# The dense stage inside attention B's loop, and elu + 1 without VectorE

## The chip, the cores and the metric

The kernel runs on one core of a Trainium2 chip. The metric is the device time of one execution in microseconds; the time before is the median of three runs. A profiled execution gives one more time, the span from the first to the last instruction, and the trace that all rows below come from.

## What is computed

Three blocks run in sequence on a batch of 32 sequences of 256 tokens with 128 features (`NB, T, P = 32, 256, 128`). Attention A ends with a linear layer, a residual, a layer norm and a two-layer MLP; an FFN of eight experts is folded into one 128 x 128 matrix per pair of sequences; attention B is an infini-attention with 16 heads of 8 features and segments of 64 tokens.

```python
# end of attention A ("dense")
out = res + _lin(out, Wf, bf)
res2 = out
on = _ln(out, g2, b2)
ffn = _lin(jax.nn.relu(_lin(on, Wr1, br1)), Wr2, br2)
return res2 + ffn

# attention B, one segment of 64 tokens, _sigma(x) = elu(x) + 1
sq = _sigma(q)
denom_q = jnp.sum(sq * z[:, :, None, :], axis=-1, keepdims=True) + EPS
A_mem = jnp.matmul(sq, M) / denom_q
scores = jnp.matmul(q, jnp.swapaxes(k, -2, -1)) * inv_sqrt_dk
scores = jnp.where(causal, -jnp.inf, scores)
A_dot = jnp.matmul(jax.nn.softmax(scores, axis=-1), v)
A_s = beta * A_mem + (1.0 - beta) * A_dot
sk = _sigma(k)
V_prev = jnp.matmul(sk, M) / denom_k
M_new = M + jnp.einsum('bhtk,bhtv->bhkv', sk, v - V_prev)
```

## The kernel before, in words

`program` calls three functions in turn, each with its own buffers, its own eight PSUM banks at most and a block of its own, and the next starts when the one before has ended: `attention_a`, `dense`, `attention_b`. They hand over through DRAM: `dense` reads the scratch tensors `y` and `ao` of attention A and the input `x`, and writes `x2`; `attention_b` reads `x2` and the folded matrices.

Every function writes one program per engine. The order of the work on an engine is the order of the code, and semaphores alone tie engines together. `pipeline` calls `body(j, u)` for one unit after another, the first and last ones written out and the middle in a loop; `active(j, u, lag)` says whether the unit `n - lag` exists, so one body holds parts of several units at different stages.

`dense` (16 units of 512 rows, names with `b_`) goes per unit: transpose `ao` (L1058), copy to `ao_t`, matmul with `Wf` into `r` (L1089, L1156), moments and norm (GpSimd, L963 to L969), normalise `z` (L1014), transpose, scale to `on`, matmul to `h` (L1099), relu to `hid` (L1042), matmul to `f` (L1112), `x1` = f + residual (L1137), a second layer norm `z1`, its transpose, the matmul with the folded FFN matrix (L1075), `x2` (L1148). Each of the intermediate results has a PSUM bank of its own.

`attention_b` (32 units of one sequence, names with `c_`) has bodies of eight steps `s`. In each step TensorE does, for one head pair g: T, the causal mask and negated row maxima (L1586) plus two heads' scores (L1591) into `t_ps`, which ScalarE turns into `prob` by exp (L1506), and one step later P times V into `c_o_bank` (L1641). At s = 1, 2, 4 and 5 a first pass of scores (L1606, L1611) goes to VectorE's row maximum (L1800), whose three bf16 parts come back through a transpose (L1712). At s = 0 to 2 of unit n the normalised x2 is transposed, multiplied to k and q (L1692, L1693) and copied to `kq` by ScalarE (L1530, L1531, the second with the factor 1/sqrt(8)). GpSimd splits `kq` into three bf16 parts (L1441 to L1444), which go to DRAM and back as the stacks `q_st` and `k_st`. The memory matrix is updated and read at s = 1 to 6 (L1671, L1677) with VectorE's divisions between (L1829, L1831, L1834, L1838). At s = 7 VectorE divides P times V by its row sums (`dinv` L1919, `ad` L1923), and three bodies later than kq come the output projection (`x3`, L1888), a layer norm, the folded matrix again (L1721) and the output (`x4`, L1906).

elu + 1 is computed as max(x, 0) + exp(min(x, 0)): VectorE takes both from PSUM (L1897, L1898), ScalarE the exp (L1546), GpSimd the sum `sg` (L1456).

`free` makes a PSUM bank's next user wait for the last reader of the user before; `USES_A` and `USES_B` list the users of a shared bank in their order within a body.

## Time and profile before

| | us |
|---|---|
| median of 3 runs (lowest, highest) | 1620.86 (1620.09, 1623.54) |
| profiled execution, its own time | 1616.4 |
| its span, first to last instruction | 1614.6 |
| attention A, up to the first load of the dense stage | 781 |
| dense stage, up to the first load of attention B | 177 |
| attention B | 657 |
| mean granted TensorE clock, share of full speed | 0.96 |

In the rows, PE is TensorE's matmul, PEld its weight load, DVE is VectorE, ACT ScalarE, POOL GpSimd. A duration includes the pipeline's latency, so neighbouring instructions of one engine overlap; a difference of two starts tells what one costs. The granted clock is 1.00 at 2.4 GHz and 0.50 at 1.2 GHz. An f32 matmul is two passes and stands as two instructions, a transpose as one.

### The profile page before, as it was taken

How to read it: one execution, taken by the hardware profiler on the slowest of the kernel's cores; microseconds unless marked ns; L12 is line 12 of the kernel's file. 1: busy time of each engine (PE TensorE's matmuls, PEld its weight loads, DVE VectorE, ACT ScalarE, POOL GpSimd, SP SyncE). 2: the span in 40 equal slices, each digit the busy share in tenths (PEclk: the TensorE clock that was granted, in tenths of full speed). 3: DMA queues.
4: the chain of work that ended last, by engine and by line, in shares of the span. 5: the costliest groups of instructions: out<-in, count | busy, mean ns of one | idle time of the engine just before them, and what ended most of it. 6: DMA issues, size and time to landing. Idle time of an engine off the chain costs nothing. (4 is left out here: it accounts for less than half of the span.)

```text
span 1614.6 us, 48196 instructions
## 1 busy us (share of the span) xinstructions
PE 1404.6 (87%) x14500; PEld 1210.9 (75%) x14564; DVE 1121.4 (69%) x3202; ACT 872.3 (54%) x2020; POOL 925.1 (57%) x1340
## 2 busy tenths in 40 slices
PE   5999999999999999999387745899899989998886
PEld 4899899898998999999266633677677766776765
DVE  4468778787888888786344535777777777777764
ACT  2466666666666666666166633444444444444441
POOL 4457676677766777764488834444444444444441
PEclk8899999999999999999599977999999999999996
DMA  4523332323322233321344413343444333333430
GB/s 133 154 86 103 99 88 81 85 88 97 97 77 79 88 97 97 87 75 30 104 115 121 117 55 92 112 108 116 115 116 111 104 104 114 110 114 116 113 101 17
DMA packets 181695, 158.13 MB, mean 98 GB/s; under 512 B 12529, under 2 KB 163185, under 8 KB 181618
## 3 DMA queue, kind: packets, MB, share of 16 engines
q1 hardware_dynamic: 181618, 157.17, 34.2%
q8 instruction: 40, 0.66, 0.2%
q14 instruction: 37, 0.30, 0.1%
HBM read 113.09 MB, written 44.04 MB: 97 GB/s over the span
## 5 line engine op out<-in xcount | busy, mean ns | idle before, releaser
L609 PE MATMUL a_bank<-a_vp,a_prob 128*128 128x74 f32 x4096 | 598.0, 253 | 0.0
L609 PEld LDWEIGHTS a_bank<-a_vp,a_prob 128*128 128x128 f32 x4096 | 587.8, 192 | 5.5
L697 DVE TENSOR_REDUCE a_nmax<-a_bank 128x2 f32<-128x512 f32 x512 | 344.9, 685 | 153.6 <-PE a_bank L578 153.3
L496 ACT ACTIVATE a_prob<-a_bank 128x512 f32<-128x512 f32 x512 | 305.3, 596 | 206.1 <-PE a_bank L593 200.8
L578 PE MATMUL a_bank<-a_k_st,a_q_st 96*128 96x256 bf16 x1024 | 260.5, 278 | 34.9 <-DVE a_nmax L697 24.4
L593 PE MATMUL a_bank<-a_q_st,a_k_st 120*128 120x256 bf16 x1024 | 281.5, 275 | 1.8 <-POOL a_q_st L345 1.8
L1641 PE MATMUL c_o_bank<-c_vb,c_prob 128*128 128x96 f32 x1024 | 178.7, 298 | 17.8 <-DVE c_ad L1923 13.9
L416 POOL TENSOR_TENSOR a_prod<-a_ov,a_wgt 128x512 f32<-128x512 f32 x128 | 151.7, 1185 | 34.1 <-POOL a_prod L416 17.2
L345 POOL TENSOR_SCALAR a_q_st<-a_mt 24x2048 bf16<-24x2048 bf16 x64 | 121.4, 1896 | 85.1 <-ACT a_mt L470 42.2
L1506 ACT ACTIVATE c_prob<-c_bank 128x256 f32<-128x256 f32 x256 | 98.8, 386 | 129.3 <-PE c_bank L1591 127.7
L578 PEld LDWEIGHTS a_bank<-a_k_st,a_q_st 96*128 96x128 bf16 x1024 | 130.7, 135 | 46.2 <-DVE a_nmax L697 32.7
L1641 PEld LDWEIGHTS c_o_bank<-c_vb,c_prob 128*128 128x128 f32 x1024 | 136.8, 194 | 34.2 <-DVE c_ad L1923 18.3
L593 PEld LDWEIGHTS a_bank<-a_q_st,a_k_st 120*128 120x128 bf16 x1024 | 140.1, 137 | 10.6 <-issue 2.2
L1441 POOL TENSOR_SCALAR c_parts<-c_kq 128x512 bf16<-128x512 f32 x32 | 19.8, 618 | 162.5 <-ACT c_kq L1531 162.5
L505 ACT COPY a_ov<-a_bank 128x292 f32<-128x292 f32 x256 | 101.6, 397 | 19.0 <-POOL a_prod L416 17.6
L1800 DVE TENSOR_REDUCE c_nmax<-c_bank 128x8 f32<-128x512 f32 x128 | 88.2, 689 | 21.2 <-PE c_bank L1611 17.7
L1423 POOL TENSOR_SCALAR c_vb<-c_vs 64x128 f32<-64x128 f32 x128 | 38.7, 302 | 96.3 <-PE c_o_bank L1641 63.3
L1591 PEld LDWEIGHTS c_bank<-c_q_st,c_k_st 128*64 128x64 bf16 x2048 | 53.0, 112 | 51.1 <-issue 39.9
L1591 PE MATMUL c_bank<-c_q_st,c_k_st 128*64 128x64 bf16 x2048 | 81.7, 203 | 0.0
L740 DVE TENSOR_REDUCE a_ao<-a_prod 128x128 f32<-128x1024 f32 x64 | 77.3, 1209 | 4.3 <-POOL a_prod L416 4.3
L1611 PE MATMUL c_bank<-c_k_st,c_q_st 128*64 128x64 bf16 x2048 | 57.0, 199 | 21.0 <-issue 16.3
L1586 PE MATMUL c_bank<-c_late,c_pick 88*128 88x256 bf16 x256 | 72.2, 282 | 0.0
(207 smaller groups left out, 2773.2 us busy)
## 6 DMA issues: line engine op xcount, KB each, us to landing
a_q_st<-scratch_a_parts_dram SPq DMA_DIRECT2D x64, 288.0 KB
a_k_st<-scratch_a_parts_dram SPq DMA_DIRECT2D x192, 96.0 KB
c_q_st<-scratch_c_parts_dram SPq DMA_DIRECT2D x64, 288.0 KB
c_k_st<-scratch_c_parts_dram SPq DMA_DIRECT2D x192, 96.0 KB
scratch_a_parts_dram<-a_parts SPq DMA_DIRECT2D x32, 384.0 KB, 2.7
scratch_c_parts_dram<-c_parts SPq DMA_DIRECT2D x32, 384.0 KB, 2.7
a_x<-in_x SPq DMA_DIRECT2D x32, 128.0 KB, 2.9
scratch_y<-a_y SPq DMA_DIRECT2D x32, 128.0 KB, 2.6
```

Source lines behind the costliest of these rows:

```text
L345: pool.tensor_scalar(q_st[o][MROW:AROWS, hs, :], mt[half_][MROW:AROWS, :].unsqueeze(1).broadcast_to([AROWS - MROW, H // 2, T]), 1.0, 0.0, ...
L416: pool.tensor_tensor(prod[o][:, gs, :].rearrange("p g (e r) -> p g e r", r=R), ov[o][:, gs, 0:RD].rearrange("p g (e r) -> p g e r", r=R), ...
L496: act.activation(prob[h % 4][:, :, :].rearrange("p a b -> p (a b)"), t_ps[h % 2][:, :], ACT.Exp).then_inc(exped, 1)
L505: act.copy(ov[(i + lag) % 2][:, 4 * g:4 * g + 4, :], o_ps[g % 2][:, 0:4 * VC].rearrange("p (g c) -> p g c", g=4)[:, :, 0:CQ]).then_inc(ov_ ...
L578: mm = pe.matmul(s_ps[t][:, hh * T:(hh + 1) * T], q_st[o][0:MROW, 2 * g + hh, t * P:(t + 1) * P], k_st[o][0:MROW, 2 * g + hh, :], start=Tr ...
L593: mm = pe.matmul(t_ps[h % 2][:, c * T:(c + 1) * T], k_st[o][0:AROWS, h, c * P:(c + 1) * P], q_st[o][0:AROWS, h, :], start=True, stop=True)
L609: mm = pe.matmul(o_ps[g % 2][:, at:at + VM], prob[h % 4][:, c, t * P:(t + 1) * P], vp[o][:, c, 0:VM], start=c == 0, stop=c == NT - 1)
L697: dve.tensor_reduce(nmax[:, t, 2 * g:2 * g + 2, 0], s_ps[t][:, :].rearrange("p (h k) -> p h k", h=2), AX.X, ALU.max, negate=True).then_inc ...
L1506: act.activation(prob[g % 4][:, :], t_ps, ACT.Exp).then_inc(exped, 1)
L1591: mm = pe.matmul(t_ps[hh * SEG:(hh + 1) * SEG, cs], k_st[st][:, 2 * g + hh, cs], q_st[st][:, 2 * g + hh, cs], start=False, stop=True, skip ...
L1641: mm = pe.matmul(o_ps[:, t, at:at + WIN], prob[g % 4][:, t * P:(t + 1) * P], vb[st][:, t, at:at + WIN], start=True, stop=True)
L1800: dve.tensor_reduce(nmax[:, t, h2 * H // 2:(h2 + 1) * H // 2], s_ps[t][:, :].rearrange("p (h k) -> p h k", h=H // 2), AX.X, ALU.max, negat ...
```

## The change

`dense` is gone as a function. Its work is written into the bodies of `dense_and_attention_b`, in units of 256 rows (one sequence), up to four bodies ahead of attention B: with `E1, E2, E3 = -4, -3, -2`, body n does the first third of unit n + 4, the second of n + 3 and the last of n + 2, and B's first layer norm takes `x2` from SBUF where it read DRAM before. The pipeline starts five bodies early (`AHEAD = 5`). All seven dense matmul and transpose groups share one PSUM bank, `d_ps`, in steps s = 1 to 7, one group a step; for that bank `c_o_bank` shrinks from two banks to one.

P times V: per head pair four matmuls, one for each segment of 64 tokens (64 stationary and 54 moving columns, even segments to output partitions 0 to 63, odd to 64 to 127), where two of 128 and 96 columns stood. The division after it is one reciprocal and one multiplication over all 128 partitions; GpSimd copies `vb` in two pieces where it took four. The factor 1/sqrt(8) moves from the copy of q into the exp, and `kq` is one copy. elu + 1 becomes max(x, 0) + min(exp(x), 1): ScalarE takes exp of `kq`, GpSimd max, min and the sum.

```diff
-        VP = 2 * 2 * (HD + 1)
-        WIN = 96
+        VP = 2 * (HD + 1)
+        WIN = 3 * VP
+        d_ps = ctx.enter_context(nc.psum_tensor("b_bank", [P, 512], F32))
-        o_ps = ctx.enter_context(nc.psum_tensor("c_o_bank", [P, NT, 512], F32))
+        o_ps = ctx.enter_context(nc.psum_tensor("c_o_bank", [P, NT, 256], F32))
+        E1, E2, E3 = -4, -3, -2
+        USES_D = [(aot_d, 1, E1), (on_d, 1, E2), (r_d, 1, E1), (hid_d, 2, E2), (z1t_d, 1, E3), (x1_d, 1, E2),
+                  (x2_d, 1, E3)]
# SyncE, at the head of a body
+                if active(j, u, -AHEAD):
...
+                    sp.dma_start(ao[1 - i][:, :, :], ao_dram[at[0], at[1]]).then_inc(ay_in, 16)
+                    sp.dma_start(dy[1 - i][:, :, :], dy_dram[at[0], at[1]]).then_inc(ay_in, 16)
+                    sp.dma_start(dx[1 - i][:, :, :], dx_dram[at[0], at[1]]).then_inc(dx_in, 16)
...
+                if active(j, u, -1):
+                    sp.wait_ge(x2_d, n + 2)
...
+                    sp.dma_start(x2_dram[at[0], at[1]], x2[1 - i][:, :, :]).then_inc(x2_out, 16)
# GpSimd: norm(0, n + 1) and dxb now at the head of a body, then vb, yb, the split, norm(1, b), and
+                    pool.tensor_scalar(pos[:, :, :], kq[i][:, :, :], 0.0, 0.0, ALU.max, ALU.add).then_inc(sg_n, 1)
                     pool.wait_ge(nexp_d, n + 1)
+                    pool.tensor_scalar(one[:, :, :], nexp[:, :, :], 1.0, 0.0, ALU.min, ALU.add).then_inc(sg_n, 1)
+                    pool.wait_ge(sg_n, 2 * (n + 1))
...
+                if active(j, u, E1):
+                    pool.tensor_tensor(xr[i][:, :, :], dx[i][:, :, :], rows(b_r2[:, :]), ALU.add).then_inc(xr_d, 1)
+                    dense_norm(0, e)
+                    pool.wait_ge(r_d, e + 1)
+                    pool.tensor_tensor(xr[i][:, :, :], xr[i][:, :, :], r[i][:, :, :], ALU.add).then_inc(xr_d, 1)
+                if active(j, u, E2):
+                    dense_norm(1, e)
# ScalarE
-                        act.copy(kq[i][:, 0, :], ps_a[:, 0:T]).then_inc(kq_d, 1)
-                        act.mul(kq[i][:, 1, :], ps_a[:, T:2 * T], HD ** -0.5).then_inc(kq_d, 1)
+                        act.copy(kq[i][:, :, :].rearrange("p a t -> p (a t)"), ps_a[:, :]).then_inc(kq_d, 1)
-                        act.wait_ge(pn_d, (n + 1) * 2)
+                        act.wait_ge(kq_d, n + 1)
-                        act.activation(nexp[:, :, :], neg[:, :, :], ACT.Exp).then_inc(nexp_d, 1)
+                        act.activation(nexp[:, :, :], kq[i][:, :, :], ACT.Exp).then_inc(nexp_d, 1)
# TensorE
-                        for t in range(NT):
+                        for c in range(NS):
                             at = g * VP
-                            mm = pe.matmul(o_ps[:, t, at:at + WIN], prob[g % 4][:, t * P:(t + 1) * P],
-                                           vb[st][:, t, at:at + WIN], start=True, stop=True)
+                            mm = pe.matmul(o_ps[c % 2 * SEG:(c % 2 + 1) * SEG, c // 2, at:at + WIN],
+                                           prob[g % 4][:, c * SEG:(c + 1) * SEG],
+                                           vb[st][:, c, at:at + WIN], start=True, stop=True)
# seven groups after P times V: s = 1 ao, s = 2 z, s = 3 r, s = 4 h, s = 5 z1, s = 6 f, s = 7 g; one of them:
+                    if s == 7 and active(j, u, E3):
+                        e = n - E3
+                        pe.wait_ge(z1t_d, e + 1)
+                        pe.wait_ge(dwc_in, (e + 1) * 16)
+                        free(pe, USES_D, 6, j, u)
+                        for t in range(NT):
+                            mm = pe.matmul(d_ps[:, t * P:(t + 1) * P], z1t[i][:, t * P:(t + 1) * P], dwc[i][:, 0, :],
+                                           start=True, stop=True)
+                        mm.then_inc(dg_p, 1)
# VectorE: r and its moments at s = 3, x1 and its moments at s = 6 behind x4, x2 at s = 7 behind ad
-                        dve.tensor_scalar(flat(pos), ps_a[:, :], 0.0, None, ALU.max).then_inc(pn_d, 1)
-                        dve.tensor_scalar(flat(neg), ps_a[:, :], 0.0, None, ALU.min).then_inc(pn_d, 1)
+                        dve.tensor_tensor(flat(x1[o]), d_ps[:, 0:T], flat(xr[o]), ALU.add).then_inc(x1_d, 1)
+                        dense_moments(1, e, x1[o])
+                        dve.reciprocal(dinv[:, :, :], out[:, :, :, HD]).then_inc(ad_d, 1)
+                        dve.wait_ge(ad_d, AD * b + 1)
+                        dve.tensor_tensor(ad[:, :, :].rearrange("q t (h e) -> q t h e", e=HD), out[:, :, :, 0:HD],
+                                          dinv[:, :, :].unsqueeze(3).broadcast_to([P, NT, H, HD]), ALU.mult
+                                          ).then_inc(ad_d, 1)
+                        dve.tensor_tensor(flat(x2[i]), d_ps[:, 0:T], flat(dxb[i]), ALU.add).then_inc(x2_d, 1)
-    dense(nc, d)
-    attention_b(nc, d)
+    dense_and_attention_b(nc, d)
```

## Rows read from the trace of the kernel before

**Rows 1.** The page's busy line, whole span: busy us, share of span, instructions.
```profile
PE 1404.6 (87%) x14500; PEld 1210.9 (75%) x14564; DVE 1121.4 (69%) x3202; ACT 872.3 (54%) x2020; POOL 925.1 (57%) x1340
```

**Rows 2.** Busy time by stretch: us, busy per engine, granted clock, DMA share, GB/s.
```profile
781.00:957.90 176.90, 126.32 (x768) 95.96 (x768) 72.48 (x304) 99.15 (x208) 130.07 (x193) 0.91 0.38 110
1041.97:1553.36 511.39, 461.17 (x5887) 357.73 (x5941) 382.39 (x1319) 233.81 (x595) 240.93 (x432) 1.00 0.39 111
1553.36:1614.62 61.26, 45.97 (x489) 35.36 (x491) 32.25 (x109) 15.27 (x39) 12.40 (x21) 0.77 0.16 44
```

**Rows 3.** ScalarE in order of time: start us, us, instruction (idle before it).
```profile
968.12 0.37 ACT L1530 COPY c_kq<-c_bank 128x256 f32<-128x256 f32 x1 [2.16 <-PE c_bank L1693]
985.62 0.37 ACT L1530 COPY c_kq<-c_bank 128x256 f32<-128x256 f32 x1 [4.71 <-PE c_bank L1693]
```

**Rows 4.** The waits, 1041.97 to 1553.36 us: waited in total, times, longest.
```profile
PE c_bank L1712 <- DVE c_mpart L1790: 13.0, 27, 0.5
PE c_o_bank L1641 <- DVE c_ad L1923: 12.6, 24, 0.5
PE c_bank L1671 <- DVE c_am L1838: 9.1, 27, 0.4
```

**Rows 5.** Chain that ended last, one body of B: start us, us, what.
```profile
1266.75 0.25 issue
1267.00 0.44 PE c_bank L1611 x16
1267.44 0.61 PE c_o_bank L1641 x4
```

**Rows 6.** TensorE in order of time, the same body.
```profile
1280.24 0.45 PE L1677 MATMUL c_bank<-c_mz,c_sg 128*128 128x144 f32 x2
1280.52 0.61 PE L1721 MATMUL c_bank<-c_wc,c_z4t 128*128 128x128 f32 x4
1280.97 0.27 PE L1586 MATMUL c_bank<-c_late,c_pick 88*128 88x256 bf16 x1
1281.42 0.69 PE L1641 MATMUL c_o_bank<-c_vb,c_prob 128*128 128x96 f32 x4
```

**Rows 7.** VectorE in order of time, the same body.
```profile
1269.92 0.69 DVE L1897 TENSOR_SCALAR c_pos<-c_bank 128x512 f32<-128x512 f32 x1 [1.25 <-ACT c_kq L1531]
1273.31 0.49 DVE L1760 BATCH_NORM_STATS2 c_stats<-c_x 128x6 f32<-128x128 f32 x2
1273.76 0.40 DVE L1764 BATCH_NORM_AGGREGATE c_mv<-c_stats 128x2 f32<-128x6 f32 x2
1280.72 0.17 DVE L1829 TENSOR_SCALAR c_dn<-c_bank 128x16 f32<-128x16 f32 x1 [0.52 <-PE c_bank L1677]
1281.78 0.42 DVE L1906 TENSOR_TENSOR c_x<-c_bank,c_xb 128x256 f32<-128x256 f32 x1
1282.14 0.74 DVE L1919 RECIPROCAL c_dinv<-c_o_bank 64x32 f32<-64x32 f32 x2
1282.92 1.01 DVE L1923 TENSOR_TENSOR c_ad<-c_o_bank,c_dinv 64x128 f32<-64x128 f32 x4
```

**Rows 8.** By tile: count, duration ns min/median/max, first and last start us.
```profile
L1058 PE MATMUL b_bank<-b_ident,b_ao x64: 272/273/476, 786.0 to 926.5; 128*128 128x128 f32 x64
L1148 DVE TENSOR_TENSOR b_x<-b_bank,b_xb x16: 691/692/692, 817.3 to 954.3; 128x512 f32<-128x512 f32 x16
L1760 DVE BATCH_NORM_STATS2 c_stats<-c_x x128: 273/282/297, 961.1 to 1606.3; 128x6 f32<-128x128 f32 x128
```

**Rows 9.** GpSimd in order of time, the same body.
```profile
1270.16 0.62 POOL L1441 TENSOR_SCALAR c_parts<-c_kq 128x512 bf16<-128x512 f32 x1 [5.01 <-ACT c_kq L1531]
1277.47 0.73 POOL L1465 TENSOR_TENSOR c_xb<-c_x,c_wc 128x256 f32<-128x256 f32 x1
1278.28 0.19 POOL L1400 TENSOR_SCALAR c_var<-c_mv 128x2 f32<-128x2 f32 x1
1279.61 0.20 POOL L1407 TENSOR_TENSOR c_shift<-c_negm,c_rs 128x2 f32<-128x2 f32 x1
```

More of the change, by code:

```diff
@@ L55, in pipeline @@
         body(n // 2, n % 2)
-    end = total // 2 - ahead
+    end = (total - ahead) // 2
     with eng.Fori(PEELED // 2, end) as j:
@@ new lines, in body @@
+                    if s == 5 and active(j, u, E3):
+                        e = n - E3
+                        act.wait_ge(z1t_p, e + 1)
+                        if later(j, e, 2):
+                            act.wait_ge(dg_p, e - 1)
+                        act.copy(z1t[i][:, :], d_ps[:, 0:T]).then_inc(z1t_d, 1)
+                    if s == 7 and active(j, u, E1):
+                        e = n - E1
+                        if later(j, e, 2):
+                            act.wait_ge(dzt_p, e - 1)
+                        dense_normed(0, e, r[i], dz[i], dz_d)
@@ new lines, in body @@
+                    if s == 5 and active(j, u, E3):
+                        e = n - E3
+                        pe.wait_ge(z1_d, (e + 1) * NT)
+                        free(pe, USES_D, 4, j, u)
+                        for t in range(NT):
+                            mm = pe.transpose(d_ps[:, t * P:(t + 1) * P], z1[i][:, t, :], ident[:, :])
+                        mm.then_inc(z1t_p, 1)
+                    if s == 6 and active(j, u, E2):
+                        e = n - E2
+                        pe.wait_ge(hid_d, 2 * (e + 1))
+                        free(pe, USES_D, 5, j, u)
+                        for t in range(NT):
+                            for c in range(2):
+                                mm = pe.matmul(d_ps[:, t * P:(t + 1) * P], hid[o][:, c, t * P:(t + 1) * P],
+                                               w_r2[:, c, :], start=c == 0, stop=c == 1)
+                        mm.then_inc(f_p, 1)
```

633 lines of the change are left out of this document (260 added, 373 removed).

## Prediction

> **What bounds the kernel now.** I read four views in this order. First the page's busy line [rows 1]: TensorE is busy for 87% of the span, so time is bought by less TensorE work or by stages in which it waits. Then the stretches [rows 2]: attention A takes the first 781 us, the dense stage has 176.9 us for itself with TensorE busy 126 of them (71%), and attention B follows to the end. Third, the eviction that starts a batch in B's loop (the copy into kq): the first is at 968.1 us, the last at 1553.36, and 27 batches lie between 1041.97 and 1553.36 [rows 2, 3], so the loop's period is 511.39 / 27 = 18.94 us. In that stretch TensorE is busy 461.2 of 511.4 us (90%), VectorE 382.4 (75%), ScalarE 46%, GpSimd 47% [rows 2]. Fourth, the waits there [rows 4]: TensorE waits in three places, for ad (12.6 us), for am (9.1) and for the row maxima's parts (13.0), per batch 0.47 + 0.34 + 0.48 = 1.29. So B's loop is bound by TensorE's order, with about 17.65 us of work per batch and 1.29 of waits for VectorE.
>
> The change therefore moves a stage that TensorE fills badly into one that it fills well. It can win only where the loop grows by less per batch than 176.9 / 32 = 5.5 us plus what the edges give.
>
> **The dense stage in the loop, TensorE.** Per batch of 256 rows: six transposes of 128 columns, eight f32 matmuls of 128 columns (2 for r, 4 for f, 2 for g), two of 256. Two f32 matmuls of 128 columns are four passes and take 1280.97 - 1280.52 = 0.45 from start to start [rows 6], 0.22 each; one of 256 columns is as long as two. A transpose is one pass (x64 for 16 units of four, rows 8), 0.11. Sum 6 x 0.11 + 8 x 0.22 + 2 x 0.44 = 3.3 us. Seven groups each begin after a semaphore; nothing before shows such a start alone. Bounds: nothing, if the sequencer runs ahead, and 0.25 each (1.75), the length of an "issue" piece in the chain [rows 5]. I take 0.25 in all, nearer to nothing, because the groups in rows 6 start without a gap after those before.
>
> **The dense stage, VectorE.** Three adds out of PSUM at 0.42 (x4's, 256 columns) and twice two statistics with their aggregates, 1273.31 to 1274.16, 0.85 [rows 7]: 1.27 + 1.7 = 3.0 us added.
>
> **elu + 1.** The max and min on VectorE go, two of 0.69 that overlap a little, some 1.3 us [rows 7]. They stand right behind the wait for kq, and the reductions, am and the maxima's parts queue behind them, for which TensorE waits. The min's work moves behind ScalarE's exp, which takes the same 512 columns as now; exp now waits for kq alone, and kq is one 512-column copy in place of two. GpSimd gets two one-input operations of 512 columns, 0.62 each by its split of kq [rows 9], and their semaphores. The sum sg is needed only by the next batch's first transposes, several us later: hidden. With these 1.3 us gone, I take the waits for am and for the parts (0.82 us) as gone: r's add and statistics come in between at s = 3, but TensorE has r, the v matmuls and the h matmuls there too.
>
> **The output of P times V.** Before, two f32 matmuls per head pair with 128 stationary and 96 moving columns, 0.61 us of the chain [rows 5], eight times. Now four with 64 and 54 columns, even and odd segments in different halves of the array. Sixteen score matmuls with 64 columns take 0.44 us in the chain [rows 5], 0.028 each, load included, which I read as two halves working at once. For f32 in that form no row exists. Upper bound: eight passes one after another, each 64/128 of the present 0.61 / 4 = 0.15 or somewhat more, again 0.61 and up to 0.07 more; lower bound: the halves fully side by side, 0.31. The group also stands next to score matmuls of the same form; the "issue" of 0.25 us where the form changes [rows 5] stays in number and only moves behind the group. I take 0.46, the middle, a gain of 0.15 x 8 = 1.2 us per batch; the ends are +0.6 and -2.4.
> The Trainium skill (TensorEngine Tiling, Key Properties) says that tiles load and multiply in parallel, and that a change of tiling mode drains TensorE. By the first alone the gain would be the whole 2.4 and the result some 36 us lower; by the second, if each group gained one more drain, nothing would be left of it. The 0.25 us pieces agree with a drain; no row shows the f32 pair.
>
> VectorE's part behind it falls from two reciprocals and four multiplications, 1282.14 to 1283.93, 1.79 us, to one of each, 0.37 + 0.45 (the multiplication has twice the columns of one of today's, so the 0.42 of an add of 256 columns is its row) [rows 7]: 0.97 us less.
>
> **The new wait.** All seven dense groups share one bank, so each waits until the one before is evicted. Six have 1.3 us or more of other TensorE work between them against an eviction of about 0.6. The tight one is x1 (s = 6) before g (s = 7). From the end of f TensorE has the memory read 0.28 (1280.24 to 1280.52), z4's matmul 0.45, the matmuls of T 0.45 (1280.97 to 1281.42) [rows 6] and P times V, some 0.4: 1.6. VectorE starts on the read's result 0.48 behind the read (1280.72), reaches x4's add 1.06 later (1281.78) [rows 7], and then has x4 and x1 at 0.42 each: 2.4. Wait 0.8; as good as nothing if VectorE gets x4 earlier, 2.4 if TensorE has nothing else, are the ends. Then VectorE's statistics (0.85), reciprocal and multiplication (0.8) end at 4.1, while TensorE needs g, the parts' transposes, T and five transposes, 0.45 + 0.25 + 0.45 + 0.6, before the first P times V of the next batch, at 4.15: the old wait for ad (0.47) is replaced. New waits 0.8 in all. ScalarE gets nine evictions or normalisations of about 0.45 (from 0.37 for 256 columns [rows 3]), 4 us, on 8.7; GpSimd four adds of 0.73, two norms of 1.53 (1278.28 to 1279.81) and the 1.24 above [rows 9], 7.2 on 8.9, minus some 0.5 for vb: 15.6 of 20.8, and its chain with gaps about 18. Both stay under the period. SyncE issues four more transfers a batch; the stack loads are behind the same split as now.
>
> **Sum for the loop.** 18.94 - 1.29 + 3.3 + 0.25 + 0.8 - 1.2 = 20.8 us. VectorE would be busy 14.2 - 1.3 - 1.0 + 3.0 = 14.9 (72%).
>
> **The edges.** The dense unit 0 starts at 786.0 and its x2 is written by 818.0; from B's first statistics (961.1) to the first kq (968.1) are 7.0 us [rows 3, 8]: 825. Counted the other way, four lead-in bodies of seven bank trips, some 1.4 us each at TensorE's lower level: 786 + 40 = 826. I take 826 for the first kq, against 968. The first interval stays 17.5 us [rows 3] (985.62 - 968.12: split, DRAM and back). The second gets 22.5, for TensorE is then likely still at 1.2 GHz in part. 26 of 20.8 = 540.8. The last three lose dense work: 20.1, 17.6, 17.3. Last kq 826 + 17.5 + 22.5 + 540.8 + 55 = 1462. From there 61.3 us now [rows 2], minus 2.3 for ad: 1521. The profiled execution had 1616.4 for a span of 1614.6, 1.8 more, and the median of the runs (1620.86) is 4.5 above that: 1521 + 6.3 = 1527 us, 5.8% less.
>
> **Rivals.** (a) P times V's halves don't overlap: +0.4 instead of -1.2, a period of 22.4; 29 x 1.6 = +46 us, 1573. For it: f32 passes were never seen in pairs. Against it: the score matmuls. 22%.
> (b) GpSimd sets the pace. It serves in order and waits three times a batch for VectorE's statistics; today it idles 5.0 us before each split [rows 9], and the additions are 6.7. Its chain of 18 plus three waits in full, 1.27 each (the 0.85 of the statistics and the 0.42 of the add before them, rows 7), gives a period of 21.8: 1527 + 29 x 1.0 = 1556. Two of the three have some us of lead as I count them. 13%. The Trainium skill (GPSIMD Engine Reference, Specifications) has GpSimd share its SBUF interface with VectorE; a stretch from that would feed this rival; no row here tells it apart.
> (c) More is hidden than I allow: full overlap in P times V and no wait at g, period 19.4, 1486. 12%.
> (d) Slower than before. The bank's turns are not covered: every one of the seven groups finds its eviction late, since ScalarE and VectorE serve in order and have other work in front. Price per group d, 7 d a batch; slower from a period of 20.8 + 94 / 29 = 24.0, so from d = 3.2 / 7 = 0.46 us. For it: the dense stage before had TensorE idle 29% with eight banks. Against it: slots of about 2.5 us of other work. 4%; with d = 0.53 it gives 1527 + 29 x 3.7 = 1634.
> That the change doesn't do its work at all is no case here: the dense stage has no stretch of its own any more.
>
> **How the numbers follow.** The forecast has 49%, with its own range 1505 to 1545; (a) 22, (b) 13, (c) 12, (d) 4. The range 1488 to 1590 leaves out (d), half of (c) and the worst of (a). Faster by over 0.2% (3.2 us, about what a measurement can tell from none): all but (d), 95%; within 0.2%: 1%; slower: 4%.
>
> **What would show it.** The spacing of kq copies: 20.8. L1641's successor: four matmuls per group, chain length near 0.46; 0.61 and more means (a). TensorE's waits for am and for the parts near zero; a wait of the g matmuls behind x1 of about 0.8 us a batch. First kq near 826. GpSimd still waiting for kq or statistics speaks against (b); r's add waiting for yb speaks for it. I'm wrong if the dense groups at s = 1 to 6 wait over 0.2 us each, or if the lead-in takes 20 us more.

## The result: 1560 us, 4% less than before, 33 us more than forecast

| | us |
|---|---|
| after, median of 4 runs (lowest, highest) | 1560.15 (1553.97, 1561.59) |
| before, in the same series, median of 4 runs | 1622.2 (1620.09, 1628.55) |
| ratio, 95% interval | 0.9604 (0.9566 to 0.9642) |
| profiled execution after, its span, mean granted clock | 1559.46, 1557.7, 0.95 |

The time lies within the range of 1488 to 1590, 15 us above the forecast's own range. The busy line of the page after, in the form of [rows 1]: TensorE is busy for 54 us less with more instructions, GpSimd for 151 us more.

```profile
PE 1350.8 (87%) x15588; PEld 1172.1 (75%) x15652; DVE 1112.1 (71%) x3058; ACT 882.1 (57%) x2068; POOL 1076.0 (69%) x1527
```

The stretches of the kernel after, as in [rows 2]. Columns: window; its length; busy time of PE, PEld, DVE, ACT, POOL with instructions; granted clock (1.00 is 2.4 GHz, 0.50 is 1.2 GHz); DMA share; GB/s. The first reaches from the dense stage's first loads to the first kq copy, the second takes the next four bodies, the third 20 bodies of the loop, the fourth one body of them, the last what follows the last kq copy.

```profile
783.00:839.43 56.43, 28.52 (x88) 19.27 (x88) 19.27 (x55) 15.75 (x38) 25.05 (x63) 0.50 0.26 76
839.43:925.37 85.94, 69.35 (x772) 52.85 (x777) 48.06 (x160) 41.56 (x101) 67.08 (x105) 0.80 0.42 116
1009.76:1447.13 437.37, 377.73 (x5519) 297.30 (x5558) 324.94 (x1080) 240.17 (x600) 354.40 (x561) 0.97 0.42 119
1294.02:1316.85 22.83, 19.84 (x277) 15.41 (x278) 16.28 (x54) 12.03 (x30) 17.82 (x29) 0.93 0.43 114
1505.10:1557.70 52.60, 35.57 (x577) 25.74 (x579) 30.73 (x95) 15.19 (x38) 15.89 (x21) 0.91 0.19 52
```

The period is 437.37 / 20 = 21.87 us where 20.8 was forecast. TensorE's waits in the third stretch, beside [rows 4] (columns: total us, times, longest; "issue" at L1454 is a matmul whose record is missing, not a wait):

```profile
PE c_bank L1618 <- DVE c_mpart L1705: 25.6, 20, 1.4
PE b_bank L1566 <- DVE b_x L1839: 24.0, 20, 1.4
PE c_bank L1454 <- issue: 10.1, 40, 0.3
```

Per batch 1.28 us for the maxima's parts (before 0.48, "gone" by the prediction) and 1.20 for x1 ahead of g (forecast 0.8); the waits for ad and am are gone. The P times V group (L1484) starts 0.35 us ahead of its successor, and 0.27 behind the start of the score group (L1454) ahead of it:

```profile
1270.32 0.44 PE L1454 MATMUL c_bank<-c_k_st,c_q_st 128*64 128x64 bf16 x16 [0.25 <-issue]
1270.59 0.42 PE L1484 MATMUL c_o_bank<-c_vb,c_prob 128*64 128x54 f32 x8
1270.94 0.44 PE L1512 MATMUL b_bank<-c_ident,b_ao 128*128 128x128 f32 x2
```

The same places before. By starts the group (L1641) took 0.52 us there and the score group (L1611) 0.37; the 0.61 of [rows 5] is a piece of the chain, not a difference of starts. In the step after it the record of the causal mask's matmul (L1606) is there, and no "issue" of 0.25 us stands ahead of L1611:

```profile
1266.43 0.32 PE L1591 MATMUL c_bank<-c_q_st,c_k_st 128*64 128x64 bf16 x8
1267.00 0.44 PE L1611 MATMUL c_bank<-c_k_st,c_q_st 128*64 128x64 bf16 x16 [0.25 <-issue]
1267.37 0.69 PE L1641 MATMUL c_o_bank<-c_vb,c_prob 128*128 128x96 f32 x4
1267.89 0.44 PE L1671 MATMUL c_bank<-c_uv,c_skn 128*128 128x144 f32 x2
...
1269.23 0.32 PE L1591 MATMUL c_bank<-c_q_st,c_k_st 128*64 128x64 bf16 x8
1269.48 0.39 PE L1606 MATMUL c_bank<-c_causal,c_ident 128*128 128x512 bf16 x1
1269.80 0.44 PE L1611 MATMUL c_bank<-c_k_st,c_q_st 128*64 128x64 bf16 x16
```

GpSimd's costliest groups in the same 20 bodies (columns: total us, mean ns). Its max and min (L1231, L1234) take 1.92 us each; the split's multiplication and addition over the same 512 columns (L1218) takes the 0.62 of [rows 9].

```profile
L1234 POOL TENSOR_SCALAR c_one<-c_nexp 128x512 f32<-128x512 f32 x20 | 38.6, 1928 | 1.6
L1231 POOL TENSOR_SCALAR c_pos<-c_kq 128x512 f32<-128x512 f32 x20 | 38.4, 1922 | 0.0
...
L1218 POOL TENSOR_SCALAR c_parts<-c_kq 128x512 bf16<-128x512 f32 x20 | 12.3, 617 | 0.0
```

And the place where the parts are late, in order of time (columns: start, duration, engine and line). VectorE reaches the first cast (L1702) at 1191.37 and needs 0.93 us for 16 columns; it ends at 1192.30, as GpSimd's subtraction (L1221, 1191.11 to 1192.26) has ended. The next cast (L1704), with GpSimd idle, takes 0.17.

```profile
1190.57 0.49 DVE L1667 BATCH_NORM_STATS2 c_stats<-c_x 128x6 f32<-128x128 f32 x2
...
1191.11 1.15 POOL L1221 TENSOR_TENSOR c_parts<-c_rest,c_parts 128x512 bf16<-128x512 f32 x1 [0.18 <-POOL c_parts L1220]
1191.37 0.93 DVE L1702 CAST c_mpart<-c_nmax 128x16 bf16<-128x16 f32 x1
...
1192.54 0.17 DVE L1704 CAST c_mpart<-c_nrest 128x16 bf16<-128x16 f32 x1
...
1192.98 0.28 PE L1618 MATMUL c_bank<-c_ident,c_mpart 128*24 128x128 bf16 x2 [1.23 <-DVE c_mpart L1705]
```

### The profile page after: what moved, and what is told of

Its sections match the earlier page's. It is cut to its first block and busy times, and to the rows that moved or that the text cites. A ratio compares the mean times of both kernels' runs of the same rounds, so it can differ in the third digit from the quotient of the medians.

```text
span 1557.7 us, 51122 instructions
## 1 busy us (share of the span) xinstructions
PE 1350.8 (87%) x15588; PEld 1172.1 (75%) x15652; DVE 1112.1 (71%) x3058; ACT 882.1 (57%) x2068; POOL 1076.0 (69%) x1527
## 5 line engine op out<-in xcount | busy, mean ns | idle before, releaser
L505 ACT COPY a_ov<-a_bank 128x292 f32<-128x292 f32 x256 | 101.6, 397 | 14.9 <-POOL a_prod L416 13.3
L1484 PE MATMUL c_o_bank<-c_vb,c_prob 128*64 128x54 f32 x2048 | 109.4, 229 | 0.6 <-ACT c_prob L1311 0.5
L1434 PEld LDWEIGHTS c_bank<-c_q_st,c_k_st 128*64 128x64 bf16 x2048 | 53.3, 112 | 52.0 <-issue 40.6
L1484 PEld LDWEIGHTS c_o_bank<-c_vb,c_prob 128*64 128x64 f32 x2048 | 82.6, 140 | 6.2 <-ACT c_prob L1311 3.9
L1454 PE MATMUL c_bank<-c_k_st,c_q_st 128*64 128x64 bf16 x2048 | 58.6, 202 | 19.3 <-issue 15.6
L1454 PEld LDWEIGHTS c_bank<-c_k_st,c_q_st 128*64 128x64 bf16 x2048 | 44.1, 115 | 32.3 <-issue 32.3
L376 POOL TENSOR_SCALAR a_parts<-a_qk 128x512 bf16<-128x512 f32 x32 | 19.8, 618 | 65.3 <-ACT a_qk L479 65.3
```

Source lines behind the costliest of these rows:

```text
L505: act.copy(ov[(i + lag) % 2][:, 4 * g:4 * g + 4, :], o_ps[g % 2][:, 0:4 * VC].rearrange("p (g c) -> p g c", g=4)[:, :, 0:CQ]).then_inc(ov_ ...
L1434: mm = pe.matmul(t_ps[hh * SEG:(hh + 1) * SEG, cs], k_st[st][:, 2 * g + hh, cs], q_st[st][:, 2 * g + hh, cs], start=False, stop=True, skip ...
L1454: mm = pe.matmul(s_ps[t][k * SEG:(k + 1) * SEG, c * SEG:(c + 1) * SEG], q_st[o][:, h, ts], k_st[o][:, h, ts], start=False, stop=True, skip ...
L1484: mm = pe.matmul(o_ps[c % 2 * SEG:(c % 2 + 1) * SEG, c // 2, at:at + WIN], prob[g % 4][:, c * SEG:(c + 1) * SEG], vb[st][:, c, at:at + WIN ...
```

## Experiments

Twelve kernels beside the kernel after; each ratio is to the kernel before, timed on the same chip. "Waits" are TensorE's, us a batch, from 20 bodies of the loop; "clock" is the granted clock there. They come from one profiled execution of each kernel; that of G, 1588 us, is the slowest of its four.

| kernel | us | ratio (95%) | period | clock | wait parts / x1 / am / ad |
|---|---|---|---|---|---|
| after | 1560 | 0.960 (0.957 to 0.964) | 21.87 | 0.97 | 1.28 / 1.20 / - / - |
| A elu on VectorE | 1546 | 0.955 (0.951 to 0.959) | 21.57 | 1.00 | 0.91 / 0.96 / 0.25 / - |
| B elu by ScalarE | 1557 | 0.961 (0.956 to 0.966) | 21.58 | 1.00 | 1.30 / 0.96 / 0.18 / - |
| C GpSimd mult, add | 1551 | 0.959 (0.954 to 0.964) | 21.88 | 0.99 | 1.28 / 1.06 / 0.38 / - |
| D GpSimd mult, max | 1564 | 0.965 (0.958 to 0.971) | 22.05 | 0.97 | 1.24 / 1.29 / - / - |
| E x1 first | 1541 | 0.951 (0.949 to 0.954) | 21.48 | 0.98 | 1.44 / - / - / 0.46 |
| F parts first | 1606 | 0.992 (0.990 to 0.995) | 23.74 | 0.88 | 0.56 / 1.83 / - / - |
| G GpSimd's order | 1578 | 0.974 (0.970 to 0.977) | 22.62 | 0.92 | 0.47 / 1.60 / - / - |
| H before + elu | 1682 | 1.041 (1.037 to 1.045) | 20.97 | 0.98 | 0.86 / no x1 / - / - |
| I before + P times V | 1577 | 0.976 (0.974 to 0.979) | 17.94 | 0.97 | 0.49 / no x1 / 0.89 / - |
| J = A + E | 1543 | 0.955 (0.954 to 0.957) | 21.68 | 1.00 | 1.20 / - / 0.47 / 0.36 |
| K = A + E + G | 1539 | 0.953 (0.951 to 0.954) | 20.88 | 1.00 | 0.46 / - / 0.40 / 0.36 |
| L = B + E + G | 1541 | 0.952 (0.948 to 0.955) | 21.03 | 1.00 | 0.47 / - / 0.75 / 0.31 |

**A. elu + 1 back on VectorE.**

```diff
-                    pool.tensor_scalar(pos[:, :, :], kq[i][:, :, :], 0.0, 0.0, ALU.max, ALU.add).then_inc(sg_n, 1)
-                    pool.tensor_scalar(one[:, :, :], nexp[:, :, :], 1.0, 0.0, ALU.min, ALU.add).then_inc(sg_n, 1)
+                        dve.tensor_scalar(flat(pos), ps_a[:, :], 0.0, None, ALU.max).then_inc(sg_n, 1)
+                        dve.tensor_scalar(flat(one), ps_a[:, :], 0.0, None, ALU.min).then_inc(sg_n, 1)
```

(ScalarE's exp then reads the min, and GpSimd's sum its result. The single copy of kq and the scale in the exp stay.)

> The kernel after, with elu + 1 as the kernel before has it: VectorE reads max(x, 0) and min(x, 0) from the bank of k, q (2 x about 0.65 us), ScalarE takes the exponential of the second, GpSimd only adds; TensorE again waits with the bank for VectorE. Theory T (GpSimd's max and min, 1.92 us each, stretch VectorE's short operations from memory to memory - the subtraction for the variance 0.64 us instead of 0.31, the first cast of the maxima's parts 0.58 instead of 0.19 - and so make MT's wait for parts 1.28 us): the stretched ones return to 0.31 and 0.19, the wait for parts falls to 0.6 to 0.9 us a batch, but VectorE carries 1.3 us more; the two roughly cancel, 1550 to 1575. Rival O (the wait comes of VectorE's order alone, the sum and the statistics of the dense stage ahead of the parts, GpSimd has no part in it): the wait for parts stays at 1.3 and VectorE's 1.3 us come on top where it is late, +20 to +40: 1580 to 1600.

1546 us: a little below even the first theory's range, and rival O's time fails. But theory T's reason fails too. Counted from the start of the kq copy, the last part is ready at 5.97 us (medians of the 20 bodies), in the kernel after at 5.96; the cast starts later and is held by the same subtraction (0.54 us). TensorE waits 0.91 instead of 1.28 for the parts because it now comes later, with a new wait of 0.25 for am. All waits together are 2.12 us instead of 2.48, and no stretch at 1.2 GHz falls into these 20 bodies. Against the kernel after the ratio is 0.9549 / 0.9604 = 0.994, which the two intervals just leave undecided.

**B. Max and min by ScalarE.**

```diff
-                        act.activation(nexp[:, :, :], kq[i][:, :, :], ACT.Exp).then_inc(nexp_d, 1)
+                        act.activation(pos[:, :, :], kq[i][:, :, :], ACT.Relu).then_inc(sg_n, 1)
+                        act.activation(one[:, :, :], kq[i][:, :, :], ACT.Relu, scale=-1.0).then_inc(sg_n, 1)
+                        act.wait_ge(sg_n, 2 * (n + 1))
+                        act.activation(nexp[:, :, :], one[:, :, :], ACT.Exp, scale=-1.0).then_inc(nexp_d, 1)
```

(GpSimd's max and min go here too.)

> The kernel after, with max(x, 0) and min(x, 0) by ScalarE (two Relu from kq, about 0.6 to 0.7 us each, then the exponential) and only the sum on GpSimd, whose busy time falls by 3.8 us a batch; VectorE's and TensorE's programs are those of after. Theory T: VectorE's stretched operations return to 0.31 and 0.19 us, the wait for parts falls from 1.28 to 0.5 to 0.8 us and that for the dense stage's x1 a little, 0.6 to 0.9 us a batch over 32 batches: 1530 to 1542. Rival O (VectorE's order alone): the waits stay, 1558 to 1563. Rival S (ScalarE, at 0.52 busy and 1.3 us more, now delays the exponentials of the scores): slower, 1565 to 1580.

1557 us. Theory T falls: 3.8 us of GpSimd less a batch, and the wait for the parts is 1.30. The cast that it blamed on max and min is held here too, by the subtraction of the split. Only the wait for x1 falls as in A, to 0.96. The loop is as fast as A's (21.58 and 21.57 us); the profiled executions differ outside these 20 bodies.

**C. GpSimd's two operations as multiplication and addition.** Leaves out the max and the min. The changed arguments of the two lines:

```diff
-kq[i][:, :, :], 0.0, 0.0, ALU.max, ALU.add    and  nexp[:, :, :], 1.0, 0.0, ALU.min, ALU.add
+kq[i][:, :, :], 1.0, 0.0, ALU.mult, ALU.add   and  nexp[:, :, :], 1.0, 0.0, ALU.mult, ALU.add
```

> The kernel after, where GpSimd's two operations are a multiplication by 1 and an addition of 0: max and min are left out, all else is issued and waited for as in after. It tells what the 1.92 us of these operations are made of, and what they cost. If the operation sets the duration (as the split of kq, multiplication and addition, has 0.62 us), both take about 0.62 us, GpSimd's busy time falls by 2.6 us a batch, and by theory T the time falls to 1535 to 1545. If the data or the second source of traffic set it, they stay at 1.9 us and the time at 1560. Rival O: 0.62 us each, and the time at 1556 to 1563.

**D. The same with max and min in second place.**

```diff
+kq[i][:, :, :], 1.0, 0.0, ALU.mult, ALU.max   and  nexp[:, :, :], 1.0, 1.0, ALU.mult, ALU.min
```

> The kernel after, with max and min as the second operation, behind a multiplication by 1, the same result. If any max or min makes GpSimd's operation slow, 1.9 us each and 1557 to 1563; if only one in first place does, 0.62 us each and the time of the kernel with a multiplication and an addition, by theory T 1535 to 1545.

The same instruction in kernel C, then in D (columns as above):

```profile
L1231 POOL TENSOR_SCALAR c_pos<-c_kq 128x512 f32<-128x512 f32 x20 | 14.1, 704 | 1.7
```

```profile
L1231 POOL TENSOR_SCALAR c_pos<-c_kq 128x512 f32<-128x512 f32 x20 | 40.2, 2010 | 1.7
```

So it is max or min in either place that makes GpSimd's operation 1.9 to 2.0 us where a multiplication with an addition has 0.70. But C's ratio can't be told from that of the kernel after, and the time lies between theory T's range and rival O's: in the merged loop most of that duration lies in GpSimd's spare time.

**E. x1's addition ahead of the second half's parts** (with its waits, moved up within step 6; its moments stay).

```diff
+                        dve.tensor_tensor(flat(x1[o]), d_ps[:, 0:T], flat(xr[o]), ALU.add).then_inc(x1_d, 1)
                         for k in range(4):
                             split_max(1, k)
                             if k < 3:
                                 read(2, k)
...
-                        dve.tensor_tensor(flat(x1[o]), d_ps[:, 0:T], flat(xr[o]), ALU.add).then_inc(x1_d, 1)
```

> The kernel after, with the dense stage's x1 addition ahead of the second half's maxima parts and the third read in step 6 of VectorE's program; its moments stay where they were. In the kernel after x1 starts 1.7 us behind the start of the third read (14.93 against 13.22 us into the body), and TensorE waits 1.2 us a batch for it. Theory Q (the period is TensorE's own passes and its two waits behind VectorE's order, so a wait taken away is won): x1 starts by 13.2, the wait falls to 0.2 or less, the second half's parts come 0.4 later and are now waited for by 0.2 us; 0.8 to 1.0 us a batch, 1530 to 1540. Rival R (the wait is given back at the next thing that VectorE or ScalarE holds, since that engine's work and not its order is short of room): the other waits grow by as much, 1553 to 1562.

1541 us, a gain over the kernel after that is clear of the noise (the intervals don't touch). The wait for x1, 1.20, is gone; 0.46 of it stands again as a wait for ad and 0.16 in the parts. The chain of waits of this kernel shows how the first comes about (columns: start, us, what): x4, x1's moments, reciprocal, multiplication, and only then P times V.

```profile
1189.93 0.42 DVE c_x L1839
1190.35 0.26 DVE b_stats L1675 x2
...
1191.04 0.37 DVE c_dinv L1855
...
1191.43 0.43 DVE c_ad L1857
1191.86 0.14 issue
1192.00 0.44 PE c_o_bank L1484 x8
```

**F. The first half's parts ahead of x3's moments.**

```diff
                         dve.tensor_tensor(flat(x3[o]), ps_b[:, 0:T], flat(xt[o]), ALU.add).then_inc(x3_d, 1)
+                    if s == 2 and active(j, u, 1):
+                        for k in range(MP // 2):
+                            split_max(0, k)
```

> The kernel after, with the first half's maxima parts (cast, subtraction, cast, subtraction) between the x3 addition and its moments, 0.8 us earlier than before. Theory H (a cast of VectorE that meets an element-wise operation of GpSimd is held until that one ends: 0.93 us instead of 0.17 beside GpSimd's last subtraction of the split of k, q): the first cast is held by 0.2 until the third operation of the split ends, the second by about 1.0 until the fourth ends, and the last part is ready only some 0.4 us earlier; TensorE's wait falls from 1.28 to 0.8 to 0.9 us: 1543 to 1552. Rival O (the operations take what they take, only their order counts): all four within 0.8 us, the wait falls to under 0.3: 1520 to 1532.

**G. GpSimd's last subtraction of the split behind the norm of x3.**

```diff
-                    split(4, pool.tensor_tensor(parts[i][:, :, 2, :], rest[:, :, :], parts[i][:, :, 1, :], ALU.subtract))
                     norm(1, b)
+                    split(4, pool.tensor_tensor(parts[i][:, :, 2, :], rest[:, :, :], parts[i][:, :, 1, :], ALU.subtract))
```

> The kernel after, with GpSimd's last subtraction of the split of k, q behind its two small operations of the norm of x3 instead of ahead of them; VectorE's program is that of after. Theory H: VectorE's first cast meets no long GpSimd operation and takes 0.17 to 0.3 instead of 0.93 us, TensorE's wait for parts falls from 1.28 to 0.5 to 0.7 us: 1537 to 1547. Rival O (the cast's duration is its own): it stays 0.93, 1557 to 1563. Rival W (GpSimd's max, min and sum come no later but the parts reach the scratch memory 1.3 us later, and the loads of the next stack with them): waits for the load of k's stack grow, 1562 to 1575.

Both slower than the kernel after, which nobody had expected. G is the clean one, since VectorE's program is untouched. Its first cast takes 0.17 us now, so theory H holds there, and the wait for the parts is 0.47. But the second half's cast, which in the kernel after mostly starts 12.1 to 13.6 us into the body, behind the sum of elu (10.8 to 12.1), now starts at 11.0 to 11.8, a few hundredths behind the start of the sum, and in 19 of 20 bodies it is held for all of it.

```profile
1151.42 0.17 DVE L1701 CAST c_mpart<-c_nmax 128x16 bf16<-128x16 f32 x1
...
1158.17 1.28 DVE L1701 CAST c_mpart<-c_nmax 128x16 bf16<-128x16 f32 x1
```

```profile
1158.14 1.27 POOL L1237 TENSOR_TENSOR c_sg<-c_pos,c_one 128x512 f32<-128x512 f32 x1 [0.17 <-POOL c_one L1233]
```

Behind it in VectorE's order stand x4 and x1, and TensorE's wait for x1 grows to 2.0 us. Right behind that wait the clock falls to 1.2 GHz. The line of the g matmuls in the body before, and two stretches of that body with their clock:

```profile
1136.83 0.70 PE L1565 MATMUL b_bank<-b_wc,b_z1t 128*128 128x128 f32 x4 [1.98 <-DVE b_x L1838]
```

```profile
1130.00:1137.30 7.30, 5.32 (x83) 4.38 (x83) 6.98 (x20) 3.04 (x9) 6.65 (x10) 1.00 0.45 128
1137.30:1147.50 10.20, 9.73 (x82) 6.48 (x82) 3.51 (x12) 4.67 (x12) 5.18 (x14) 0.50 0.47 144
```

Undisturbed bodies of G have 20.9 to 21.4 us, no longer than those of after (21.3 to 21.5); those with 7 to 10 us at 1.2 GHz have 24 to 25. So the edit gained a few tenths in the undisturbed bodies, and the clock took more than it gave. In F it went in 14 of 20 bodies as theory H had it: the first cast took 0.5 us at most, the second 1.1, held by the fourth operation of the split. In 5 bodies the first cast met that operation (1.0 us). The last part was ready 0.5 us earlier than in the kernel after (5.42 against 5.96, medians), and the wait fell to 0.56. But the second half's cast met the sum as in G (1.24 us), and the wait for x1 rose to 1.83. Of F's expectation theory H was right about the hold and wrong about the time, since neither theory had the second hold or the clock.

**H. The kernel before with the elu part alone** (and what goes with it: one kq copy, the scale in the exp).

> The kernel before with the elu part of the change alone (one copy of k, q, the scale in the exponential, max and min by GpSimd, the sum as before); the dense stage stays behind the loop and P times V as it was. As the prediction had it: VectorE loses 1.3 us a batch, and TensorE's waits for am and for the parts of the maxima, 0.82 us a batch, go: 27 x 0.82 = 22, about 1598. Theory H, with the kernel after faster by 14 us when VectorE does the elu: GpSimd's two 1.92 us operations hold VectorE's short ones by as much as the 1.3 us relieve it: 1615 to 1630.

1682 us, 63 more, far outside both. Its waits over 20 bodies:

```profile
PE c_bank L1593 <- ACT c_prob L1512: 28.9, 20, 1.6
PE c_bank L1716 <- DVE c_mpart L1794: 17.2, 20, 1.0
PE c_bank L1684 <- DVE c_mz L1820: 16.0, 20, 0.8
```

1.45 + 0.86 + 0.80 = 3.1 us against 1.29 before. The first: GpSimd serves in order, so with 3.84 us of max and min in front the norm of the next layer norm (L1407) comes at 1312.52. ScalarE has idled 3.52 us for it, and the exp of a score group queues behind z:

```profile
1312.52 0.20 POOL L1407 TENSOR_TENSOR c_shift<-c_negm,c_rs 128x2 f32<-128x2 f32 x1
...
1312.75 0.88 ACT L1564 ACTIVATE c_z<-c_x,c_shift,c_rs 128x128 f32<-128x128 f32 x2 [3.52 <-POOL c_shift L1407]
...
1313.94 0.28 PE L1593 MATMUL c_bank<-c_late,c_pick 88*128 88x256 bf16 x1 [1.55 <-ACT c_prob L1512]
```

The third: the addition into mz meets the sum and takes 1.37 us (0.31 before). The second shows best why VectorE's 1.3 us bought nothing. The cast in the kernel before, and in H:

```profile
1273.11 1.16 POOL L1444 TENSOR_TENSOR c_parts<-c_rest,c_parts 128x512 bf16<-128x512 f32 x1 [0.18 <-POOL c_parts L1443]
...
1274.11 0.18 DVE L1787 CAST c_mpart<-c_nmax 128x16 bf16<-128x16 f32 x1
```

```profile
1302.12 1.16 POOL L1444 TENSOR_TENSOR c_parts<-c_rest,c_parts 128x512 bf16<-128x512 f32 x1 [0.18 <-POOL c_parts L1443]
...
1302.73 0.58 DVE L1791 CAST c_mpart<-c_nmax 128x16 bf16<-128x16 f32 x1
```

Before, VectorE arrived 0.16 us ahead of the subtraction's end. Freed of max and min it arrives earlier and is held until the same end: the last part is ready 5.68 us after the start of the kq copy before and 5.62 in H. And TensorE, which no longer waits for am, stands at the transposes earlier, so its wait for the parts grows.

**I. The kernel before with the P times V part alone** (the `-` and `+` lines of TensorE's and VectorE's P times V in the diff above, and two copies of vb by GpSimd where it took four).

> The kernel before with P times V as the change has it (one group of eight 64-column passes per step into one bank, one division, half the constants of ones) and nothing else: elu on VectorE, the dense stage behind the loop. In the kernel after such a group takes 0.35 us from its start to the next group's, where the prediction took 0.46 and the kernel before has 0.61; the division is 0.82 us of VectorE instead of 1.79, and the wait for it (0.47 us a batch) is gone. Theory Q (what TensorE no longer does is won): 8 x 0.26 + 0.47 = 2.5 us a batch, 80 us: 1535 to 1550. By the prediction's sizes (8 x 0.15 + 0.47 = 1.7, 53 us): 1560 to 1570. Rival R (the time is given back in the waits for VectorE's parts, reads and am, whose chain stays as long): 1575 to 1600.

1577 us, 38 less: the time of rival R, but only in part its reason. The wait for ad (0.47) went, that for am rose from 0.34 to 0.89. And TensorE's own work fell by less than theory Q's 2.1 us: 17 of the 20 bodies have 17.57 us, less 1.38 of waits 16.2, against 17.65 before. The other three have a stretch at 1.2 GHz and take 20 us.

```profile
PE c_bank L1669 <- DVE c_am L1836: 17.7, 20, 0.9
```

**J. A with E.**

> The kernel after with elu + 1 on VectorE as in the kernel before, and the dense stage's x1 addition ahead of the second half's parts. Elu on VectorE alone gave 1546, x1 first alone 1541. Theory Q (both act on their own: GpSimd's short queue on one, TensorE's wait for x1, 0.96 us a batch in the kernel with elu on VectorE, on the other): 1520 to 1532. Rival R (both had removed the same wait): 1538 to 1546. Rival C (the shorter waits are paid back by stretches at half clock, as in the kernels with the parts first and with GpSimd's order changed, where 16 to 20 such stretches of 7 to 10 us stood in the loop): 1545 or more.

**K. J with G.**

> The same, and GpSimd's last subtraction of the split of k, q behind the norm of x3. With GpSimd's max and min in place this order moved the long hold (0.93 us) from the first half's cast to the second half's (1.28 us beside the sum), which made TensorE's wait for x1 2.0 us and the clock fall: 1578. Theory H (VectorE's short operations are held only by a GpSimd operation of both sources or of the same memory that runs beside them): without max and min the sum is over by about 8.6 us into the body, the second half's cast at about 12 meets nothing, the first takes 0.17 us, the wait for the first parts falls from about 1.2 to 0.5 us; 12 to 22 us below the kernel with x1 first: 1503 to 1518. Rival C (the clock): not below it, 1525 to 1545. Rival R (only moved to the next wait): within 5 us of it.

**L. K with the elu of B.**

> The kernel with x1 first and GpSimd's order changed, and elu's max and min by ScalarE (Relu of kq and of its negative, then the exponential) instead of VectorE. It tells whether VectorE's 1.3 us still count once its holds beside GpSimd are gone. With elu on VectorE this order has an undisturbed period of 20.77 to 20.96 us, with waits for am of 0.50, for the maxima's parts 0.45 and for ad 0.35 us a batch, all of them behind VectorE's chain, whose first link in a body are the two readings of the bank (1.3 us). Theory V (that chain sets these waits): without the two the wait for am goes and that for the parts falls by some tenths; 0.6 to 1.0 us a batch, 1510 to 1525. Theory G (VectorE's place in the chain is fixed by TensorE's scores, ScalarE's 1.3 us more cost as much): 1534 to 1542. Rival S (ScalarE's exponentials of the scores come later, TensorE waits for them): 1545 or more. In all of them the last batches pay about 8 us for the later parts of k.

J gives rival R: 1543, no better than A or E alone. The wait for x1 (0.96 in A) is gone and 0.29 + 0.22 + 0.36 = 0.87 stands for parts, am and ad instead. The parts are later because GpSimd is: it begins the split 1.53 us behind the start of the kq copy (A 1.20, before 0.92), its last subtraction ends at 5.65 (A 5.31), and the cast is held until then. K's loop shows theory H again, now with nothing left to collide with: parts 0.46, period 20.88, clock 1.00. Its time, 1539, is still outside theory H's 1503 to 1518. Its waits, then those of L:

```profile
PE c_bank L1615 <- DVE c_mpart L1702: 9.1, 20, 0.5
PE c_bank L1572 <- DVE c_am L1750: 8.0, 12, 0.8
PE c_o_bank L1478 <- DVE c_ad L1860: 7.2, 20, 0.5
```

```profile
PE c_bank L1575 <- DVE c_am L1750: 15.0, 20, 1.0
...
PE c_bank L1615 <- DVE c_mpart L1702: 9.4, 20, 0.7
PE c_o_bank L1481 <- DVE c_ad L1854: 6.1, 20, 0.4
```

16 us over 20 bodies were won against J, and 4 arrived (2 in the profiled executions, where these rows are from). What follows the last kq copy takes 61.1 us at a clock of 0.72, against 53.3 at 0.84 in J; the two intervals before it are 3.4 longer, and the loop's 20 bodies start 2.7 later. In the last 100 us stand 5.4 us of waits for the stack of k (0.4 in J), which is loaded behind the split's last part:

```profile
1473.29:1534.40 61.11, 44.41 (x580) 31.04 (x579) 29.91 (x97) 15.23 (x38) 12.06 (x19) 0.72 0.15 45
```

```profile
PE c_bank L1443 <- DMA c_k_st<-scratch_c_parts_dram: 5.4, 3, 3.0
```

L bears out theory G: without VectorE's 1.3 us the wait for am is longer, not shorter, and the time is the same (1541). E, K and L end at 0.951 to 0.953, the best versions found, all about 1% below the kernel after; which of them is best isn't resolved.

## Why the prediction was right in direction and 33 us low

**What bounds the kernel: right.** TensorE's order with a few waits bounds the loop, and it wins because a stage that filled TensorE badly moved in. Split by experiments: P times V 0.976 (I), then the dense stage in the loop, with the single kq copy, 0.955 / 0.976 = 0.978 (A over I), then elu off VectorE 0.960 / 0.955 = 1.006 (after over A). The third part of the change returned nothing that can be told from noise.

**TensorE's work in the loop: 1.1 us too high.** Forecast 17.65 + 3.3 + 0.25 - 1.2 = 20.0 us. Measured: the 13 of the 20 bodies without a stretch at 1.2 GHz have 21.35 us, less 2.47 of waits 18.9. From start to next start, waits taken out, the groups of a batch compare so with the kernel before: P times V 4.43 to 2.89, the score groups 3.60 to 2.91, the dense groups 3.9 new (forecast 3.55 with their starts), the rest 0.4 less, mostly the memory's matmuls. The term that was mis-sized is P times V: a gain of 2.2 us with the score groups, where I took 1.2. Its own part, 0.52 to 0.35 by most starts, is near my 0.15; the 0.1 that the score group ahead of it gained each time (0.37 to 0.27 in the rows above) I had at nothing. Kernel I, with this part alone, shows the same two (3.23 and 2.79 us are left). Rival (a) is out: eight passes in 0.35 us leave no room for one after another.
I had said that the "issue" of 0.25 us where the form changes stays. It is no cost of a form: it is the unrecorded matmul of the causal mask, as the rows before with and without L1606 show. The 0.25 that bounded a group's start was the same piece. The drain that the Trainium skill (TensorEngine Tiling, Key Properties) states for a change of tiling mode added nothing for the new group here; that a score group of 64 columns is followed 0.1 us sooner by a group of 64 columns than by one of 128 agrees with it. The seven group starts have no row of their own, and no group at s = 1 to 6 waits regularly.

**Waits for am and parts "as gone": this step failed.** The step took VectorE's 1.3 us off the chain and called 0.82 us of waits gone. am's is gone in the kernel after, but the parts' went from 0.48 to 1.28. In medians of the loop, counted from the start of the kq copy: VectorE reaches the first cast at 4.34 us instead of 4.85, and is then held by GpSimd's last subtraction, which ends at 5.31 instead of 5.03. So the last part is ready at 5.96 instead of 5.70, while TensorE, with no wait for am, stands at the transposes 0.5 us earlier. G takes only the hold away: ready at 5.15, and the wait is 0.47. I had the row for the cast's place in VectorE's order and never laid GpSimd's timeline beside it. The prediction's sentence that no row tells a stretch from the shared interface apart was true of the rows chosen, and the mechanism was filed under GpSimd's pace as the bound of the period, which it isn't. GpSimd's order does act on it: two copies of vb and the dense stage's addition of yb now stand ahead of the split, which begins 1.19 us behind the start of the kq copy (before 0.92), and the later it begins, the later the hold ends (J).
The Trainium skill (SBUF — State Buffer, SBUF: two separate sides) has one port pair that GpSimd shares with VectorE's instructions in a 2-port mode or with two SBUF inputs; whichever starts first has it for the whole instruction, and the other blocks. By that rule a held cast ends with GpSimd's operation, and the trace agrees: it took 0.93, 0.54 (A) and 1.28 us (G), each time ending within 0.05 us of it; that the cast runs in a 2-port mode no row shows. The trace doesn't agree beside GpSimd's max of 1.92 us: the addition into mz, with two SBUF inputs, began 0.11 us behind it, took 0.67 instead of 0.31 and was over 1.15 us ahead of it.

**The new wait for x1: mechanism right, size off.** 1.20 instead of 0.8, and E shows that it was VectorE's order. That it replaces the wait for ad was right too: E takes it away and ad's comes back at 0.46.

**GpSimd: operation mis-sized, consequence right by luck.** Two operations of 0.62 were forecast, 1.92 is measured; it is busy 354.4 / 20 = 17.7 us a batch instead of 15.6. Rival (b), that it sets the pace, doesn't hold for the merged loop (B and C: no change outside the intervals). The prediction's sign for that was a wrong one: GpSimd still waiting for kq was to speak against (b), and in these 20 bodies it never does, since it comes to the split late. In the kernel before the same edit costs 63 us (H) by GpSimd's order, with GpSimd busy for 61%: the merged kernel has that norm at the head of a body, behind a wait of its own.

**VectorE's work: right where it isn't held.** The division is 1203.20 to 1204.01, 0.81 us. It is busy 324.94 / 20 = 16.2 us a batch where 14.9 was forecast; the first cast's 0.76 and the 0.36 of mz's addition, both held, are most of the difference.

**The edges.** First kq copy 839 instead of 826: the lead-in runs wholly at 1.2 GHz. Its first transposes come 2.7 us later than the dense stage's did (788.8 against 786.0), TensorE waits 5.9 us for the load of b_y ahead of the second body, and seven bank trips take 14.0 us (822.8 to 836.8), 2.0 each instead of 1.4; against that, 21 trips stand in it and not 28. From first to last kq copy 665.7 instead of 636: 20 x 1.07 = 21 from the period, 3 in the last intervals, the rest in the fourth body, 26.95 us with a mean clock of 0.77. After it 52.6 instead of 59.0. Together 13 + 30 - 6 = 37 on a span of 1521.

**The clock: not in the sum of the loop.** It takes 21.87 - 21.35 = 0.5 us a batch there. In the 20 bodies every fall begins within 2.6 us behind the end of a long wait of TensorE, mostly the longest of the body: in the kernel after about 2 us behind one of 1.40 us for the parts, in G 0.5 to 2.0 us behind the 1.98 us wait for x1, in H 1.5 to 1.8 behind one of 1.55 for the exp. So a wait that a fall follows is dearer than its length: in the kernel after by 1.5 us in 7 bodies of 20, in G by about 3 to 4. That the wait causes the fall is argued from this order in time, not shown.

**Luck in the total.** Carried over 29 intervals, the waits cost about 49 us more than forecast (1.7 a batch) and the clock 15, and TensorE's work 32 less. That these partly cancel is luck; the total is nearer than its terms. And rival (c)'s period of 19.4 doesn't follow from its own terms, 20.8 - 1.2 - 0.8 = 18.8, or about 19.3 with the wait for ad back, as E has it.

**What stays open.** Which waits the clock falls behind. Of the nine waits of 1.39 us and more in the kernel after it falls behind seven, and behind none of about 1.23. But B has nine of 1.41 and 1.42 and no fall in 20 bodies, E has eight of 1.43 to 1.48 without a fall and six of 1.41 to 1.47 with one, H falls behind three of its ten of about 1.55, and I falls behind two waits of 0.89 and 0.49. Whether elu off VectorE costs the last half per cent or nothing isn't settled either.

## What to carry to other kernels

Before counting time taken off an engine's queue as won, find the next thing that queue meets: another engine's long operation that holds it, a transfer, or a later wait; in the kernel before 1.3 us off VectorE moved its next result by 0.06 (H). When work is given to an engine in order, list what stands behind it and who waits for that, even if the engine is half idle. And judge an order by the undisturbed period and the granted clock separately, since a better order can be the slower kernel.

## What the runs showed of the hardware

- GpSimd's tensor_scalar with max or min, f32, 512 columns: 1.92 to 2.01 us; with multiplication and addition 0.62 (bf16 out) to 0.70 us (f32 out).
- Casts of VectorE from SBUF, and its subtractions and additions with two SBUF sources, are held by a GpSimd operation that began before: 16 columns in 1.28 us beside a two-source sum of 1.27, 144 columns in 1.37 (0.31 alone). Casts that began within 0.01 us of GpSimd's operation took 0.16. VectorE's statistics, and what it reads from PSUM, weren't: the statistics at 1190.57 above take their 0.49 beside GpSimd's work as before [rows 7]. Beside the 1.92 us max, mz's addition took 0.67 us and did not last to that operation's end.
- Four pairs of f32 matmul passes of 64 by 54 on the two halves of the array: 0.35 us from start to next start, against 0.52 for four passes of 128 by 96.
